# Output stores by tile from ScalarE's queue, and the w_out load one chunk earlier, in an eight-core transformer-layer kernel

## The reference, cut to what matters

```
flat   = layernorm(x)
shared = swiglu(flat @ w_in.T) @ w_out.T
w_se   = top-2 expert weights of each token (softmax of group and expert logits), else 0
h      = swiglu(flat @ w1.T)
routed = sum over e of (h * w_se[:, e]) @ w2[e].T          # 8 experts, all computed densely
out    = x + shared + routed
```

## Time and profile before

| | us |
|---|---|
| two executions timed | 4695.47 and 5282.37, median 4988.92 |
| profiled execution | 4687.35 |
| its span on the slowest core (core 5) | 4686.3 |
| spans of the eight cores | 4658.8 to 4686.3 |
| TensorE busy on core 5 | 3851.2 (82%) |
| VectorE busy | 1091.7 (23%) |
| ScalarE busy | 515.1 (11%) |
| mean granted TensorE clock, core 5 | 0.910 |

### The profile page before, as it was taken

One profiled execution on the slowest core, in us unless ns is written; L12 is line 12 of the kernel. 1 busy time (PEld: TensorE's weight loads), 2 busy tenths in 40 slices (PEclk: granted clock), 3 DMA queues, 4 the chain that ended last, 5 costly groups with the idle time before them and its releaser, 6 DMA issues.

```text
span 4686.3 us, 46733 instructions; the slowest of 8 cores (4658.8 to 4686.3 us)
## 1 busy us (share of the span) xinstructions
PE 3851.2 (82%) x17976; PEld 1708.9 (36%) x17976; DVE 1091.7 (23%) x2177; ACT 515.1 (11%) x789; POOL 123.3 (3%) x234
## 2 busy tenths in 40 slices
PE   3568622259995789999889999969999996999998
PEld 1223211024442334444334444434444443444443
DVE  0150310125453211222321122231122223111111
ACT  1110110124442101000110000011000001010000
POOL 0000000000000000000000000000000000000000
PEclk8769866679997899999899999989999998999999
DMA  5330699971211133222132322113132211322121
GB/s 90 78 120 0 70 121 118 119 120 55 64 55 64 57 101 135 81 81 81 41 99 74 120 81 92 70 50 135 46 144 81 81 41 68 117 63 109 72 89 56
DMA packets 70874, 391.17 MB, mean 83 GB/s; under 512 B 9712, under 2 KB 9712, under 8 KB 58880
## 3 DMA queue, kind: packets, MB, share of 16 engines
q0 software_dynamic: 24480, 253.88, 22.6%
q1 hardware_dynamic: 45184, 134.23, 8.7%
q10 hardware_dynamic: 992, 0.07, 0.0%
HBM read 423.81 MB, written 88.08 MB: 109 GB/s over the span
## 4 chain that ended last, share of the span: by engine, by line
PE 75%; DMA 7%; another core or an unknown queue 7%; DVE 5%; issue 2%; ACT 2%; DVEq 1%; POOL 0%; ACTq 0%; POOLq 0%; SPq 0%
PE ps_r L1099 19%; PE ps_tb L1099 19%; PE ps_a L1016 4%; PE ps_tb L1016 4%; PE ps_r L1023 4%; PE ps_b L1023 4%; DMA w<-w2s 3%; PE ps_kv L355 3%; PE ps_r L1066 3%; PE ps_tb L1066 2%; PE ps_id L355 2%; PE ps_id L511 2%; PE ps_q L355 2%; PE ps_tr L555 1%
## 5 line engine op out<-in xcount | busy, mean ns | idle before, releaser
L1099 PE MATMUL ps_r<-w,hsT 128*128 128x512 bf16 x4096 | 914.2, 382 | 31.1 <-DMA w<-w2s 31.1
L1099 PE MATMUL ps_tb<-w,hsT 128*128 128x512 bf16 x4096 | 904.9, 379 | 0.0
L1099 PEld LDWEIGHTS ps_r<-w,hsT 128*128 128x128 bf16 x4096 | 402.7, 98 | 522.3 <-issue 45.4
L1099 PEld LDWEIGHTS ps_tb<-w,hsT 128*128 128x128 bf16 x4096 | 400.8, 98 | 483.3
L355 PE MATMUL ps_kv<-wtk_b,xT_b 128*128 128x512 bf16 x512 | 133.7, 421 | 304.5 <-ACT xT_b L352 304.5
L1016 PE MATMUL ps_a<-hiT,wab 128*128 128x512 bf16 x1024 | 247.7, 398 | 136.4 <-DMA wab<-wabs 128.8
L1107 DVE SCALAR_TENSOR_TENSOR acc<-ps_tb,wse,acc 128x1024 f32<-128x1024 f32 x128 | 164.3, 1284 | 719.7 <-PE ps_tb L1099 719.7
L1107 DVE SCALAR_TENSOR_TENSOR acc<-ps_r,wse,acc 128x1024 f32<-128x1024 f32 x128 | 164.3, 1284 | 667.6 <-PE ps_r L1099 667.6
L1023 PE MATMUL ps_r<-hiT,wab 128*128 128x512 bf16 x1024 | 231.4, 379 | 1.1 <-DMA wab<-wabs 1.1
L1016 PE MATMUL ps_tb<-hiT,wab 128*128 128x512 bf16 x1024 | 231.4, 379 | 0.2 <-issue 0.2
L1023 PE MATMUL ps_b<-hiT,wab 128*128 128x512 bf16 x1024 | 231.5, 379 | 0.0
(11 more groups left out here) (203 smaller groups left out, 2635.7 us busy)
## 6 DMA issues: line engine op xcount, KB each, us to landing
w<-w2s POOLq DMA_DIRECT2D x72, 2048.0 KB, 13.1
w2s<-w2T POOLq DMA_DIRECT2D x8, 4096.0 KB, 375.4
wab<-wabs POOLq DMA_DIRECT2D x128, 256.0 KB, 3.3
wab<-wabs SPq DMA_DIRECT2D x128, 256.0 KB, 2.6
xf<-xp SPq DMA_DIRECT2D x32, 512.0 KB, 3.4
xf<-x SPq DMA_DIRECT2D x32, 512.0 KB, 4.1
x1s<-x_sb SPq DMA_DIRECT2D x32, 512.0 KB, 4.9
x1t<-x1s SPq DMA_DIRECT2D x32, 512.0 KB, 9.2
```

The source lines that it names most:

```text
L1099: mi = PE.matmul(pr[:, 512 * h:512 * (h + 1)], hsT[:, hc * CH + i * 128: hc * CH + (i + 1) * 128], w2_b[bi][:, hc * D + 512 * h: hc * D + ...
```

## The change

The 4 MB store at a chunk's end becomes eight stores of 512 KB, one for each tile. Each is issued from ScalarE's queue, right after the last expert's VectorE operation on that tile. `s_out` therefore counts 128 a chunk in place of 16, and SP no longer waits for `sv_fin` at a chunk's end. The w_out load of chunks 1, 2 and 3 is issued on POOL at the end of the chunk before, behind the load of expert 7, once expert 6 is done; chunk 0's stays where it was.

```
+                def wout_load(cc):
+                    kw2 = cc * 9
+                    bw2 = kw2 % 2
+                    if kw2 == 0:
+                        PL.wait_ge(s_cvt, CVT)
+                    if kw2 >= 2:
+                        a2, j2 = divmod(kw2 - 2, 9)
+                        PL.wait_ge(st_r, a2 * RPC + (j2 + 1) * TPC)
+                    for h2 in range(2):
+                        PL.dma_start(w2_b[bw2][:, h2 * 8 * D:(h2 + 1) * 8 * D],
+                                     w2s_d.ap()[0, :, h2 * 8 * D:(h2 + 1) * 8 * D]
+                                     ).then_inc(s_w2[bw2], 16)
...
                     if kind == 0:
                         if c > 0:
-                            SP.wait_ge(s_out, 16 * c)
+                            SP.wait_ge(s_out, 128 * c)
                             SP.wait_ge(sv_fin, c)
                         SP.dma_start(acc3, x1r[c], ).then_inc(s_ac, 16)
                         kw = c * 9
                         bw = kw % 2
-                        if kw == 0:
-                            PL.wait_ge(s_cvt, CVT)
-                        if kw >= 2:
-                            cc, jj = divmod(kw - 2, 9)
-                            PL.wait_ge(st_r, cc * RPC + (jj + 1) * TPC)
-                        for h2 in range(2):
-                            PL.dma_start(w2_b[bw][:, h2 * 8 * D:(h2 + 1) * 8 * D],
-                                         w2s_d.ap()[0, :, h2 * 8 * D:(h2 + 1) * 8 * D]
-                                         ).then_inc(s_w2[bw], 16)
+                        if c == 0:
+                            wout_load(0)
...
                         DVE.engine_nop().then_inc(sv_acc, 1)
+                        if e == NE - 1:
+                            ACT.wait_ge(sv_acc, n_r)
+                            ACT.dma_start(out_t4[c, i], acc[:, i * D:(i + 1) * D]
+                                          ).then_inc(s_out, 16)
+                if c + 1 < NCH:
+                    wout_load(c + 1)
                 DVE.engine_nop().then_inc(sv_fin, 1)
-                SP.wait_ge(sv_fin, c + 1)
-                SP.dma_start(out_r[c], acc3).then_inc(s_out, 16)
-            SP.wait_ge(s_out, 16 * NCH)
+            SP.wait_ge(s_out, 128 * NCH)
```

More of the change, by code:

```diff
@@ L819, in build_nc @@
             out_r = out_d.ap().rearrange("(ch tl p) d -> ch p tl d", p=128, tl=TPC)
+            out_t4 = out_d.ap().rearrange("(ch tl p) d -> ch tl p d", p=128, tl=TPC)
             x1r = x1s_d.ap().rearrange("(ch tl p) d -> ch p tl d", p=128, tl=TPC)
```

## The result

The ratio of the changed kernel's time to that of the kernel before is 0.9937, 95% interval 0.9906 to 0.9968: 0.6% faster. The forecast, 4655 us from 4687.35, was 0.9931. The profiled execution took 4654.02 us. More than half of all executions of either kernel run with the cores of one or both dies at a lower granted clock and take up to 5384 us, which the ratio leaves out. The plain median of 28 executions, which holds them all, is 4882.72 us (before: 4991.35, 27 executions), and this lies outside the range 4632 to 4686 that I gave.

A forecast was written before the change was run, and what follows sets the result against it. The chain ending last, 75% TensorE and 7% DMA, was taken to bound the kernel, so only its waits or tail count. 23.6 (w_out waits) + 9.1 (tail) = 32.7 us off 4687.35 gave 4655 us, range 4632 to 4686.

The forecast's parts named there:

- The w_out term: TensorE's waits ahead of w_out in chunks 1 to 3 fall to a floor of 3.07 us each, saving 23.6 us.
- The clock: First w_out tiles stay slow after the shorter gap; taken as 0, with a balance between -0.5 and +5.0 us.
- Rival (b): More comes back: 5.0 us of clock and 6 us, half the boundary's 12.1, giving 4644 us; 11%.
- `acc` taken as hidden: The `acc` load lands within 25.9 us of issue, before w_out's third tile needs it; nothing lost.
- Rival (a): w_out waits for `acc` instead: 8.9 us come back, the clock may cost 5.5, giving 4669 us; 12%.
- The boundary: Between chunks, an earlier first group saves 0, since the third group waits for VectorE's gates; bounds 0 to 12.1 us.
- ScalarE: The 32 store issues on ScalarE's queue cost 0, ending 0.66 us before its next copy is due.
- Rival (c): A store holds ScalarE until it lands, costing 11 us and giving 4666 us; 4%.
- The tail: At the program's end only the last tile's 512 KB store follows VectorE, landing in 2.63 us; 9.1 us saved.
- The sum: Over the whole kernel, w_out waits 23.6, tail 9.1 and three terms of 0 make 32.7 us, 0.7%.
- Rival (d): Slower: `wab` pieces come late in the 128 groups; 0.33 us each gives 4697 us, 1.0 gives 4783; 5%.
- (e): Something other than the load, say `hsT`, held w_out's start; only the tail's saving remains, 4678 us; 4%.

The follow-up runs named there:

- e1: The changed kernel with its stores put back on SP as one 4 MB store, so only the w_out load is early; ratio 0.9956 to the kernel before.
- e3: The kernel before, with the first two `a` pieces of the next chunk issued on SP ahead of the 4 MB store; ratio 1.0001.
- g_after: The changed kernel with the gates moved from ahead of kind 0 to behind every second product of kind 0; ratio 0.9651 to the kernel before.
- e2: The kernel before with the eight stores by tile on ScalarE's queue, the w_out load left late; ratio 0.9984.
- l_early: The changed kernel with chunk 0's w_out load and every chunk's expert-0 load issued behind kind 0's second `b` piece; ratio 0.9866 to the kernel before.

## Why the prediction was right, and where it was not

- *The w_out term, 23.6 us: mechanism right, size that of one core.* The floor was met in all three chunks, 9.2 us in all for 3 x 3.07. But the term was worked out on core 5, which before had the longest waits of all (45.4 us; the others 36.2 to 44.1). On the average core the three moved loads' waits went from 28.4 to 9.3 us: 19.1 saved, while chunk 0's, not moved, went from 11.3 to 11.7. e1 gave 0.44%, 20.6 us.
- *The clock, 0: right on the slowest core, with some luck.* There 8.75 us three times against 8.34 to 8.97; the sum of the excess was 5.0 us and is 5.5, as taken from the row with the gap of 3.44. But a gap of 3 us costs the clock in some cases only: 20 of 24 first tiles here, 13 of 24 in e1 (in the kernel before, behind gaps of 8.1 us and more, all 24). The mean of eight cores, three first tiles together, went from 26.7 to 24.9 us, so 1.8 us came back, and 3.2 in e1. Rival (b) comes true by that much.
- *`acc` taken as hidden: right,* 14.2 to 15.5 us to landing against the 25.9 allowed. (By the prediction's own clock term the first tile lasts 8.75 us and not 6.91, which allows 27.8.) Rival (a) falls with e1.
- *The boundary, 0: right,* by e3, and by g_after for the reason given. The other half of rival (b) falls here.
- *ScalarE, 0: right.* 1.37 us before and after; an issue took 0.338 us, not the 0.508 of a smaller transfer. Rival (c) falls.
- *The tail, 9.1 us: right.* 12.0 to 2.9 us; stores landed in 2.7 us in the median, against 2.63 taken. e2: 0.16% or 7.5 us, 9.1 within its interval.
- *The sum, 32.7 us, against 33.3 between the two profiled executions: closer than it deserves.* On the mean of the eight cores the spans fell by 31.1 us. Of that, 19.1 are the moved loads, 9.1 the tail and 1.8 the clock; another 2.7 arise before chunk 0's first group (its `glog` came at 1505.1 us on average before and at 1502.4 after), where nothing was changed. The remaining 1.6 us went the other way; 1.0 of them are longer waits for chunk 0's w_out load and the loads of expert 0. That `glog` came at 1511 to 1515 us in the experiments that leave everything ahead of it alone, and among the cores of one execution it spreads over 11 to 15 us, so it moves by itself. The slowest core is not the same one in the two executions either. So agreement to 0.6 us is luck. The ratio's interval, 15 to 44 us, holds both 30.0 (the three terms) and 32.7.
- *Rival (d)* did not come: waits for `b` and later `a` pieces stay under 1 us. *(e)* falls with e1.
- *The step that failed is the last one: which time was forecast, and the range.* The prediction notes that the two executions timed before lie 12% apart and that their median, 4988.92 us, "lies where neither ran". It then forecasts "what compares with the lower", and the range adds up the change's own terms and the 8 us between two like executions. What set 5282.37 apart from 4695.47 us was put at nothing, without a reason. The runs showed that it is in most executions and far larger than any term of the sum. Of the 28 of the kernel after, eight took 4651 to 4658 us and lie in the range, two took 4696 and 4698, and 18 took 4772 to 5378; so the median is 4882.72. (Before, nine of 27 took 4683 to 4707 us and 18 took 4787 to 5384.) Why an execution is one of the longer ones stays open; no run here separates it. As a forecast of the median, 4632 to 4686 was too narrow by far; as one of the ratio it held. A slip besides: the low end takes off 6 us for a difference that the text gives as 8; nothing hangs on it.

## What to carry to other kernels

A load that a buffer is free for, but that stands behind other loads in a queue in program order, is worth moving up to where the buffer comes free; the gain ends at the floor set by the compute chain at the same place, and that floor can be read off before (here 3.07 us of 11 on the core read). When a wait ended by a DMA goes, look at what that DMA was itself waiting for and at the next wait behind it: three waits of about 2 us were worth nothing while a chain of gates held the group after next, and taking that chain off was worth 120 us. Look too at what is being loaded at the place a load is moved to: l_early's two loads cost about 14 us there. Read a term on all cores before giving it the size that the slowest core shows. And where executions timed beforehand lie 12% apart, say which of them is forecast and give the range a term for it.

## What the runs showed of the hardware that I had not expected

A gap of 3 us on TensorE can cost as much clock as one of 11, and need not. Behind gaps of 2.96 to 3.29 us, 20 of 24 first tiles of 32 matmuls in the kernel after took 8.45 to 8.59 us from start to start, 13 of 24 in e1, and the others 6.90, the full rate. Behind gaps of 8.1 to 11.2 us none of 24 ran at the full rate, and behind gaps of 2.75 us (l_early) 25 of 32 did. A single row, here the one behind a gap of 3.44 us, does not tell such a price. And two transfers of 4 MB side by side took about as long as one behind the other would have: 27.8 to 31.7 us for `acc` beside w_out in the kernel before, 14.2 to 15.5 us alone in the kernel after.
